# A macaron block in one launch: the second feed-forward stage's first loads moved into the output stage, and a new order of loads at the join before it

## The reference

```python
x = x + 0.5 * ffn(layernorm(x), weight, bias, lora_A, lora_B, starts)   # x is 2 x 1024 x 1024, float32
x = x + mla_attention(layernorm(x), wq_a, q_a_ln_w, wq_b, wkv_a, kv_a_ln_w, wkv_b, wo)
x = x + 0.5 * ffn(layernorm(x), weight, bias, lora_A, lora_B, starts)
```

## Time and profile before

| | us |
|---|---|
| median of three runs | 1924.73 |
| the three runs | 1918.6, 1924.73, 5604.57 |
| the profiled execution | 1922.07 |
| its span, first to last instruction | 1919.9 |
| PE busy in the span | 1809.1 (94%) |
| DVE, ACT, POOL busy | 1233.0, 998.3, 870.5 |

### The profile page before, as it was taken

How to read it: one execution, slowest core, us unless ns; L and a number is a source line. 1 busy time by engine, 2 the same in 40 slices (tenths; PEclk the granted TensorE clock), 3 DMA queues, 4 the chain that set the end, 5 groups by cost and what they waited for, 6 DMA issues and landing times. The chain is left out here.

```text
span 1919.9 us, 44288 instructions
## 1 busy us (share of the span) xinstructions
PE 1809.1 (94%) x15472; PEld 1420.9 (74%) x15472; DVE 1233.0 (64%) x2653; ACT 998.3 (52%) x2135; POOL 870.5 (45%) x641
## 2 busy tenths in 40 slices
PE   6999959899999999999999999997799999969999
PEld 3778859877777777777777777775688888857887
DVE  5565348788898888988889898887422111125553
ACT  2211047788887888878788787885311000012210
POOL 2232111377777878778787777873000000014321
PEclk9999979999999999999999999999899999979999
DMA  6542152311212212121121212213643332225321
GB/s 221 179 154 98 66 164 94 83 59 52 85 60 75 65 53 79 56 84 51 67 79 56 80 50 72 72 65 127 204 132 96 103 107 87 66 110 175 121 90 64
DMA packets 111698, 182.48 MB, mean 95 GB/s; under 512 B 27473, under 2 KB 64465, under 8 KB 109585
## 3 DMA queue, kind: packets, MB, share of 16 engines
q1 hardware_dynamic: 111632, 181.61, 29.5%
HBM read 122.06 MB, written 59.51 MB: 95 GB/s over the span
## 5 line engine op out<-in xcount | busy, mean ns | idle before, releaser
L1194 PE MATMUL psS<-keyT,q 128*128 128x512 f32 (+2 forms) x2304 | 472.0, 350 | 23.9 <-POOL q L570 14.1
L1194 PEld LDWEIGHTS psS<-keyT,q 128*128 128x128 f32 x2304 | 380.2, 189 | 118.1 <-DVE negmax L1311 42.4
L1261 ACT ACTIVATE prob<-prob,negmax 128x640 f32<-128x640 f32 (+7 forms) x512 | 392.0, 767 | 78.2 <-DVE negmax L1311 75.6
L1321 DVE STREAM_TRANSPOSE pT<-prob 128x640 f32<-128x640 f32 (+7 forms) x512 | 379.9, 762 | 66.5 <-PE psV L1211 61.7
L1311 DVE CUSTOM_DVE_ANT_0 prob<-psS,mask 128x640 f32<-128x640 f32 (+7 forms) x512 | 371.7, 742 | 19.7 <-PE psS L1194 6.2
L421 PE MATMUL f_psy<-f_weff,f_xT 128*128 128x512 f32 x1344 | 313.5, 392 | 0.0
L1007 PE MATMUL psS<-o_w,o_o 128*128 128x512 f32 x1344 | 304.8, 389 | 0.0
L1007 PEld LDWEIGHTS psS<-o_w,o_o 128*128 128x128 f32 x1344 | 252.3, 188 | 52.4
L421 PEld LDWEIGHTS f_psy<-f_weff,f_xT 128*128 128x128 f32 x1344 | 250.8, 188 | 53.7 <-issue 1.7
L1211 PE MATMUL psV<-pT,val 32*64 32x512 f32 (+3 forms) x8192 | 265.8, 408 | 7.2 <-DVE pT L1321 6.2
L1211 PEld LDWEIGHTS psV<-pT,val 32*64 32x64 f32 x8192 | 169.2, 132 | 111.2 <-issue 67.3
(11 more groups left out here) (113 smaller groups left out, 1914.9 us busy)
## 6 DMA issues: line engine op xcount, KB each, us to landing
wo<-in_wo SPq DMA_DIRECT2D x16, 1024.0 KB, 5.8
pT<-row_scales SPq DMA_DIRECT2D x128, 128.0 KB, 2.9
oT<-pT SPq DMA_DIRECT2D x64, 256.0 KB, 2.5
o_in<-oT SPq DMA_DIRECT2D x32, 512.0 KB, 5.3
f_xt<-in_x SPq DMA_DIRECT2D x16, 512.0 KB, 4.3
f_w_in<-in_w SPq DMA_DIRECT2D x16, 512.0 KB, 6.2
w_sum<-f_w_in SPq DMA_DIRECT2D x16, 512.0 KB, 5.3
x<-f_xo SPq DMA_DIRECT2D x16, 512.0 KB, 3.0
```

Of the source, the lines that this page charges most:

```text
L1194: ins = nc.tensor.matmul(psS[:, slot, start + x0:start + x1], q[:, e, a, t * P:(t + 1) * P], k.keyT[:, m, b * S + x0:b * S + x1], start=(i ...
L1261: nc.scalar.activation(row, row, ACT.Exp, bias=negmax[:, n % 8:n % 8 + 1], scale=-1.0, accum_out=rowsum[:, column(n, s):column(n, s) + 1]) ...
L1321: nc.vector.transpose(pT[:, n % 2, t, 0:width], prob[:, n % RING, 0:width]).then_inc(turned, 1)
```

## The change

1. **Feed-forward 2 starts in the output stage.** A new class `Early` places the four weight slots and the first two tokens' buffers of feed-forward 2 over buffers that the output stage has given up (`o_w_in` and `o[0]`). SP loads the four weight pieces once all 16 output weight pieces are split, and the two token tiles once tile 14's product is done. DVE and ACT compute statistics and normalise both tiles before tile 15's result.
2. **The last stores are waited for later.** SP no longer waits for the `x2` stores at the end of the block. In feed-forward 2, SP waits for them before the bias load, POOL before the first bias addition and ACT before piece 1 (`vacated`).
3. **New order of loads at the attention's end.** SP loads output weight pieces 0 to 3 one half-step earlier, tile 0's outputs as soon as their last store has landed, and then tile 1's outputs and pieces 4 to 7 before the row scales of the last half. ACT and DVE split eight pieces instead of four before they copy and join the last values. Tile 1 follows eight pieces behind tile 0 instead of four (`behind`).
4. Buffers of both feed-forward stages are allocated in another order.

```diff
-def ffn_phase(nc, tag, k, src_d, dst_d, bias_d, sum_d, w_d=None, adapters=None):
+def ffn_phase(nc, tag, k, src_d, dst_d, bias_d, sum_d, w_d=None, adapters=None, early=None):
...
+        def vacated(eng):
+
+            if early is not None:
+                for j in range(2):
+                    eng.wait_ge(early.x_stored[j], 16 * NT // 2)
...
-            load_w(0)
-            load_x(1, 1)
+            if early is None:
+                load_w(0)
+                load_x(1, 1)
+            vacated(sp)
             sp.dma_start(bias_half[:], bias_d.rearrange("(a n) -> a n", a=1).to_broadcast([P, D])).then_inc(bias_in, 16)
-            for i in range(1, SLOTS):
-                load_w(i)
+            if early is None:
+                for i in range(1, SLOTS):
+                    load_w(i)
...
             pieces_low([0])
             pool.wait_ge(halved, 1)
+            vacated(pool)
             add_bias(0, 0)
...
+                    if early is not None and i == 1:
+                        vacated(act)
...
+class Early:
...
+    def load_weights(self, sp):
+        for i in range(SLOTS):
+            sp.dma_start(self.w_in[:, i, :], self.sum_d[i * P:(i + 1) * P, :]).then_inc(self.w_loaded[i], 16)
+
+    def load_tokens(self, sp, src_d):
+        for n in range(2):
+            sp.wait_ge(self.x_stored[n], 16)
+            sp.dma_start(self.front.xt[:, n, :], src_d[n * P:(n + 1) * P, :]).then_inc(self.front.x_in[n], 16)
...
     def sync_steps(self, sp):
+        sp.wait_ge(self.w_lo, PAIRS)
+        self.early.load_weights(sp)
+
...
+                if not later(n, NT) and n == NT - 1:
+                    sp.wait_ge(self.product, 2 * NT - 2)
+                    self.early.load_tokens(sp, self.dst_d)
...
         output_steps(sp, step)
-        for j in range(2):
-            sp.wait_ge(self.y_stored[j], 16 * NT // 2)
...
-            if pair in (0, 1, 4, 5):
-                self.outputs_lo(nc, dve, pair // 4, pair // 4, pair % 2)
+            if pair in (0, 1, 8, 9):
+                self.outputs_lo(nc, dve, pair // 8, pair // 8, pair % 2)
...
+            if not later(n, NT) and n == NT - 1:
+                for m in range(2):
+                    self.early.front.stats_of(nc, dve, m, m, loads_of(m, m))
+                    self.early.front.normalise(nc, dve, m, m)
...
-        behind = 4
+        behind = 8
...
-                    if r.last and s == 1 and (job, n) == ("X", 0):
+                    if r.last and s == 0 and (job, n) == ("X", 1):
                         sp.wait_ge(q_done, 4 * units)
                         sp.wait_ge(w_stored, 16 * (units - 2))
                         output.load_weights(sp, range(SLOTS))
-                    if r.last and s == 1 and job == "Z":
+                    if r.last and s == 0 and (job, n) == ("Y", 1):
+                        sp.wait_ge(w_done, units)
                         sp.wait_ge(o_stored[0], 16 * (units - 1))
                         output.load_outputs(sp, 0)
-                    if r.last and s == 1 and (job, n) == ("X", 1):
-                        output.load_weights(sp, range(SLOTS, 2 * SLOTS))
+                    if r.last and s == 1 and job == "Z":
                         sp.wait_ge(output.o_lo, 2)
                         output.load_outputs(sp, 1)
+                        output.load_weights(sp, range(SLOTS, 2 * SLOTS))
...
                             output.weights_hi(nc, act, range(SLOTS))
+                            act.wait_ge(turned, TILES * units)
+                            output.weights_hi(nc, act, range(SLOTS, 2 * SLOTS))
...
-                            output.weights_lo(nc, dve, range(SLOTS))
+                            output.weights_lo(nc, dve, range(2 * SLOTS))
```

More of the change, by code:

```diff
@@ L115, with __init__ @@
 class Front:
[L118 to L121, removed]
+    def __init__(self, c, tag, overlaid=False):
+        if not overlaid:
+            self.xt = c.sb(tag + "xt", [P, 2, D])
+            self.xn = c.sb(tag + "xn", [P, 2, D])
+            self.turns_into(c, tag)
         self.st = c.sb(tag + "st", [P, 2, 12])
@@ L468, in _ @@
                 choose()
-            f.stats_of(nc, dve, 0, 0, loads_of(0, 0))
-            f.normalise(nc, dve, 0, 0)
+            if early is None:
+                f.stats_of(nc, dve, 0, 0, loads_of(0, 0))
+                f.normalise(nc, dve, 0, 0)
             if w_d is not None:
@@ L502, in _, with __init__ @@
             ffn_steps(dve, step)
+class Early:
+    def __init__(self, c, sum_d):
+        self.sum_d = sum_d
+        self.front = Front(c, "f2_", overlaid=True)
+        self.home = -(-c.nc.sbuf_base // 32) * 32
+        self.w_in = c.nc.alloc_sbuf_tensor_at("f2_w_in", [P, SLOTS, D], F32, offset=self.home)
+        self.front.place(c.nc, "f2_", self.home + 4 * D * SLOTS)
+        self.w_loaded = [c.sem(f"f2_w_loaded{j}") for j in range(SLOTS)]
+        self.x_stored = [c.sem(f"o_y_stored{j}") for j in range(2)]
+    def load_weights(self, sp):
[5 more added lines that the diff above has]
+            sp.dma_start(self.front.xt[:, n, :], src_d[n * P:(n + 1) * P, :]).then_inc(self.front.x_in[n], 16)
 class Queries:
@@ L901, in __init__ @@
         self.product, self.result = c.sem("o_product"), c.sem("o_result")
-        self.y_stored = [c.sem(f"o_y_stored{j}") for j in range(2)]
+        self.y_stored = early.x_stored
+        self.early, self.eps = early, eps
     def half_of(self, h):
@@ L1043, in attention_phase @@
         w_done, w_copied, w_stored = c.sem("w_done"), c.sem("w_copied"), c.sem("w_stored")
-        output = Output(nc, c, {**k.homes, **c.homes}, psS, src_d, dst_d, oT_d, wvo_d)
+        output = Output(nc, c, {**k.homes, **c.homes}, psS, src_d, dst_d, oT_d, wvo_d, k.early, k.eps_ln)
         units = 2 * PAIRS
@@ L1295, in _ @@
             rounds(act, body)
-            act.wait_ge(turned, TILES * units)
-            output.weights_hi(nc, act, range(SLOTS, 14))
+            output.weights_hi(nc, act, range(2 * SLOTS, 14))
             for ch in range(2):
@@ L1366, in _ @@
             rounds(dve, body)
-            output.weights_lo(nc, dve, range(SLOTS, PAIRS))
+            output.weights_lo(nc, dve, range(2 * SLOTS, PAIRS))
             output.vector_steps(nc, dve)
@@ L1431, in macaron_block @@
         ffn_phase(nc, "f1_", k, x, x1_d, bias, sum_d, w, (lora_a, lora_b, starts))
+        k.early = Early(c, sum_d)
         with ExitStack() as inner:
@@ L1441, in macaron_block @@
             attention_phase(nc, k, (wn, wpe, wv, wo), oT_d, rinv_d, wvo_d, v_d, x1_d, x2_d)
-        ffn_phase(nc, "f2_", k, x2_d, out, bias, sum_d)
+        ffn_phase(nc, "f2_", k, x2_d, out, bias, sum_d, early=k.early)
 class Shared:
```

45 lines of the change are left out of this document (31 added, 14 removed).

## The result

| | us |
|---|---|
| before, median of six runs (1918.60 to 5604.57) | 1924.55 |
| changed, median of six runs (1910.13 to 1914.22) | 1911.95 |
| ratio, 95% interval | 0.9944 [0.9934, 0.9954] |
| profiled execution: before, changed | 1922.07, 1914.22 |
| its span: before, changed | 1919.9, 1912.2 |

The kernel became 0.56% faster, 8.8 to 12.7 us by the interval, and the forecast was 14.6. The run of 5604.57 us is left out of the ratio, which compares only runs close to the fastest of their kernel. The profiled execution of the changed kernel is the slowest of its six; against the profiled one of before the gain is only 7.85.

The account below looks back on a forecast made before the run. PE was taken as full except in a few stretches, two of them at the joins, the second bound by when the bias is halved. 1922.07 - 2.1 (first join) - 12.5 (second join) = 1907.5 us; range 1901 to 1914.

Parts of the forecast that it names:

- rival (a): Second join: the low clock takes the place of the POOL chain, 5.9 us lost, 1913.4 us in all; chance 0.15.
- First join, place and chain: Attention's end: PE runs 48 matmuls, then waits for piece 8, whose load stands behind stores and joins; resumes at 1361.4.
- The 0.9 us that were added for POOL beside DVE: First join, before piece 8: POOL's scaling lengthened by 0.9 us while DVE works on two SBUF inputs.
- First join, size: Attention's end to the single tiles' end: 1395.9 against 1398.0, a gain of 2.1 us.
- what the low clock after such a gap costs: First join, behind the wait at piece 8: 1.75 us added to the 32.8 us of 144 matmuls.
- without a gap: First join: PE does eight pieces of tile 0, 48 matmuls in 10.9 us, with no wait until 1351.2.
- Second join, halved bias: Start of feed-forward 2: bias halved at E + 9.6 instead of 22.1, the 23.75 us behind it unchanged; gain 12.5 us.
- E: Start of the output stage's last result, 1702.84 in the kernel before; second-join times are counted from it.
- (e): Second join: early loads do nothing if the last stores still hold the block's opening; 2.3 us later, 1909.8; chance 0.06.
- (b): Both joins: transfers land faster, first join gives 6.9 us, second 13.4; 1901.8 us; chance 0.12.
- (d): First join: kernel slower than before if piece 7 lands at about 1359.5 or later, 23 us after issue; chance 0.03.
- (c): First join gives nothing, the stall at piece 8 eats all; 1909.6 to 1910 us; chance 0.12.

Follow-up runs that it names:

- the last kernel: Changed kernel with four pieces and last row scales moved ahead, feed-forward 1 buffers as before, tile 1 before piece 1: 1898.63 us median, 0.9874 against the kernel before.

## Why the prediction was right, and where it was not

Range and class held; the forecast of 1907.5 was 4.5 us low against the median and 6.7 against the profiled execution, to which its sum was made (1914.22, just above the range). The mechanism of both joins was right. That the median still fell in the range is in part luck: its upper end had been set for rival (a) and for differences between runs, and what used it up was a cost that the prediction did not know. By its steps:

- **First join, place and chain: right.** From the values' start, forecast and measured: piece 7 landed 15.6 and 15.8, joins begun 17.9 and 18.0, scaling done 24.9 and 25.2, piece 8 landed 29.9 and 30.0, PE resumed 32.1 and 32.45. The 0.9 us that were added for POOL beside DVE are there: 3.58 against 2.60. The DVE instruction beside it lasts 1.23 us and overlaps it by 1.12.
- **First join, size: 1.1 instead of 2.1.** The term "what the low clock after such a gap costs" was 1.75 and measured 2.4 (35.13 against 32.72 at a granted clock of 1.00); with the 0.35 above that makes the difference of 1.0. The same term was 1.4 to 2.7 in the eight traces of this order, so most of this miss is the spread of a price that was taken from one trace. A further 1.14 us wait inside the 48 matmuls ("without a gap") cost nothing, since piece 8 ended the wait behind them. What was not looked for is that the chain had a cheap cure: four pieces ahead of the joins, and above all the row scales' place on SP.
- **Second join, halved bias: 11.7 instead of 12.5.** The block opened at E + 1.50, as forecast. Halving at E + 10.6 instead of 9.6: tile 1's transposes took 1.94 us instead of 1.0, the granted clock being 0.51 in 1710 to 1720. That is part of rival (a), for 1 us and not 5.9. Two other kernels with this join as changed had the transposes at 1.16 and 1.17 us, and there the first two tiles ended at E + 33.1 and 33.3, where the forecast was 33.3. From halving to the end 23.6, forecast 23.75. But the low clock was left out of the sum with the argument that PE is ready at E + 13 and piece 2's low part comes at E + 15.3. That was wrong about PE: it was ready at E + 15.9 (1722.51), and the low part came at 16.3. At the low clock PE's path is nearly as long as POOL's, the waits for POOL are down to 0.2 to 0.5 us, and halving the bias 2.7 us earlier gave 0.3. The sum came out because POOL's chain was still the longer one, by 0.2 to 0.5 us and not by 2.3.
- **Item 4, "in another order": no term at all, measured 5.0 us in the trace.** This is the largest error and nearly the whole difference. It was taken as a rearrangement without instructions, so without cost; the kernel with the places alone shows about 4 us for each feed-forward stage at the distance of 7 x 4096 + 192 bytes.
- **Rivals.** (e) is excluded: the first transposes started 1.50 us after E, and with the wait put back 3.84. (b) and (d) did not come: landings were as forecast. (c) did not come either, by the traces: the first join gives 0.8 to 1.9 us. (a) came in its mechanism, at 1 us of its 5.9; the rest of what the low clock costs lay in the shadow of POOL's chain.

## What to carry to other kernels

A change of allocation order is a change: compare the duration of the same uninterrupted group of matmuls in each stage before and after, and if it moved, try a few other distances between the two operands. When a wait is removed at a hand-written join, follow the new last wait back to the queue it stands in; here one pair of small transfers behind six large loads cost about 6 us (0.9930 against 0.9899), several times what the whole reordering of the join had won. A forecast through one engine's chain should name the second longest path and its distance, since that is what a further change will meet.

## What the runs showed of the hardware that was not expected

- The rate of fp32 matmuls of 128x512 depends on how the two operands lie to each other in a partition: 11.14 to 11.18 us for 48 at distances of 41 x 4096, 7 x 4096 and 7 x 4096 + 256 bytes, 11.45 at 7 x 4096 + 192, 2.8% more, with a granted clock of 1.00 from 160 to 220 us in both kernels and no wait shown.
- A gap of 10.03 us in PE's work brought the granted clock to 0.50 until 5 us after work had resumed, and cost 2.4 us over 144 matmuls; over all traces gaps of 7.5 to 12.6 us cost 1.4 to 2.7. In the kernel whose gaps there were 0.34, 1.99 and 0.57 us the clock stayed at 1.00. But a gap of 1.84 us at the second join was followed by 0.50 from 1725 to 1728, and one of 1.83 in the last kernel by nothing: short gaps go either way.
- In the second join, where PE works in short groups with waits of 1.5 to 3.6 us between them, the granted clock fell to 0.50 at a different place in each execution: from 1710 to 1719 in the changed kernel, from 1716 to 1722 where the bias is halved first, from 1725 to 1728 where tile 1 comes before piece 1, and nowhere in the last kernel, which has the same order there as the one before it. What decides was not settled.
- VectorE and POOL, both with inputs in SBUF, can lengthen each other by nearly as long as they overlap: POOL's two scalings took 3.58 us (once 3.59) instead of 2.60 beside a DVE instruction of 1.23, in all eight kernels with this order, and with the bias halved first DVE's low part of 1.22 us took 2.19 where it began 1.1 us before POOL's addition ended. Not every overlap does it: in the changed kernel POOL's low part at 1743.40 took its usual 2.40 us although DVE began its own low parts at 1744.30.
